# A graph network on one core: VectorE's turn in another order, node work in smaller pieces, the first steps rearranged

## The chip, the core and the metric

One core of a Trainium2 chip runs the whole network. The metric is the device time of one execution in microseconds; less is better. The engines are TensorE (PE in the profile; PEld is its weight load), VectorE (DVE), ScalarE (ACT), GpSimd (POOL) and SyncE (SP, whose queue issues most DMAs). They run side by side and meet through semaphores alone.

## What is computed

3125 nodes with 128 features each, 53,125 edges sorted by target. Four graph layers, each after a layer norm with ReLU:

```python
x[dst] gets, per edge:  relu([x[src], x[dst], edge_attr] @ mW1 + mb1) @ mW2 + mb2   # layer 0, then the mean
upd = relu([x, agg] @ uW1 + ub1) @ uW2 + ub2 + x ; layer norm with gamma, beta      # layer 0
x @ W1 + b1 + (segment_sum(x[src]) @ W2 + b2)                                       # layer 1
segment_sum(norm * (x @ W3)[src]) + bias      # layer 2, norm from edge weights and degrees
relu(0.9 * segment_sum(norm * x[src]) + 0.1 * x) + x                                # layer 3
```

## The kernel before

Nodes are 25 tiles of 128. The 53,125 edges are 104 quads of 512 (four columns of 128). Because the edges are sorted, the 512 targets of quad q lie in a window of 128 nodes that begins at first(q), about 30 q.

**Prologue (to about 30 us).** For the seven tile groups j, VectorE makes `variance(0, 0, x)(j)` and then `norm(0, 0)(j - 1)`; ScalarE makes the root between them; GpSimd scales the rows (`normed_rows`, L795, 25 operations); TensorE transposes them (T0) and multiplies with the first message weights (P, `make_P`); ScalarE reads P, and SP stores it as `p_rows` (L581). Meanwhile src, dst and weights of the edges are turned to float, packed and stored as `edges_in_order` by VectorE, GpSimd and SP, and `idx`, the source of every edge, comes to its place (L1235).

**Sweep (104 quads, loop `for q in range(NQ)` on every engine).** Layer 0 messages, and at the same time the dense blocks of the adjacency for layers 1 to 3:
- GpSimd gathers the rows of P for the sources of the edges: four indirect DMAs a quad (L811), into G, a ring of six quads (GS = 6). It waits only for the indices, for all of P stored, and from quad 6 on for the messages of quad q - 6.
- TensorE adds the gathered rows and the window's Q rows in PSUM (`pre`, L1736 and L1737), sums the messages by one-hots (`seg`, L1750), makes the Q window of quad q + 4 (L1723), and multiplies the operands of block step u = q - 4 (`blocks`, L1767 and L1769), one half before `seg` and one behind the Q window. It goes in this order: pre(q+1), blocks(u, 0), seg(q), Q window, a node piece if SLOT has one, blocks(u, 1).
- ScalarE reads messages (L951) and block products (L976, L981) and makes the rows of the windows (L957, L964).
- VectorE's turn q: add the sums of quad q - 1 into ST (L1284), copy the Q window out of PSUM (L1291), make the four one-hots of quad q + 1 (L1297), and the operands of block step u = q - 2: the mask (L1308, `iota_k` against the keys), the low keys (L1311), and three products of the mask with the parts of the weights (L1315). Then the steps of node pieces.
- The dense update of layer 0 is cut into 12 node pieces g (11 of two tiles in the sweep, the last of three tiles after it). SLOT gives each one three places: A at quad BEGIN + APART g, U two quads later, V five later; `piece_steps` lets variance, norm, residual, second norm and the low part follow the V by 2 to 7 quads. BEGIN is 57 and APART 4. At quad 46 one operation adds a bias to all of h (L1372), at quad 50 one to all of x (L1376), and degrees are made at quads 8, 16, 24, 32 (`block_degrees`) and 40.

```python
                if 8 <= q < 40 and q % 8 == 0:
                    block_degrees(q // 8 - 1)
                if q == 46:
                    bias_h0(0)
                if q == 50:
                    bias_x(B_BE)
```

**After the sweep.** The last piece is finished, GpSimd and others widen the count blocks from bytes (L502), and TensorE goes through the dense products of layers 1, 2 and 3 (L1896, L1911) to the end.

The order on each engine is the order in which the code is written; nothing reorders it.

## Time and profile before

| | us |
|---|---|
| median of 3 runs | 927.59 (924.33 to 929.0) |
| profiled execution | 929.52 |
| its span, first to last instruction | 927.7 |
| first gather to last gather starts | 25.82 to 600.15 |
| TensorE busy, share of span | 91% |
| VectorE busy | 68% |
| GpSimd busy | 56% |
| mean granted TensorE clock | 0.950 |

The profile is one execution, taken by the hardware. A row of the timeline gives start, length, engine, line, operation, output<-input, and in brackets how long the engine was idle before and what ended that. Numbers of buffers are left out of names: `room` is one large region that holds G, the Q rows, the operands and the window rows; `ps` is PSUM. TensorE's operations overlap, so its busy time says little; an engine that isn't the limit may idle at no cost.

### The profile page before, as it was taken

The numbers are of one execution on the slowest core, as the hardware profiler recorded it, in microseconds if no ns is written. First come the engines' busy times: TensorE is split into PE (matmuls) and PEld (weight loads), VectorE is DVE, ScalarE is ACT, GpSimd is POOL, SyncE is SP. The second block draws the span as 40 slices with busy tenths as digits, with TensorE's granted clock in tenths as the row PEclk, the third lists the DMA queues.
The fourth block names the chain that finished last, engine by engine and source line by source line (L and its number), as shares of the span: only waits on it lengthen the run. The fifth ranks groups of instructions, "written<-read, shape, count | busy, mean of one in ns | idle before, by whom it ended". The sixth has DMA issues, their size and how long they took to land.

```text
span 927.7 us, 18932 instructions
## 1 busy us (share of the span) xinstructions
PE 845.5 (91%) x6949; PEld 788.6 (85%) x6949; DVE 632.2 (68%) x1747; ACT 506.6 (55%) x1005; POOL 522.3 (56%) x496
## 2 busy tenths in 40 slices
PE   4549889898988789999989999989999999999996
PEld 4549888897988789998989999968899888898886
DVE  7659968976987777788987899748843311117663
ACT  4226666765766547677767878833444011114864
POOL 8677777777777787777777777753110000005110
PEclk9679989988999889999999999989999999999998
DMA  6624555656655655665655556582146877686500
GB/s 192 160 71 130 163 158 168 209 156 212 188 169 172 139 173 165 181 196 176 180 168 169 168 168 195 177 257 71 45 178 254 313 286 290 236 301 207 163 24 28
DMA packets 104977, 163.68 MB, mean 176 GB/s; under 512 B 14699, under 2 KB 65426, under 8 KB 104879
## 3 DMA queue, kind: packets, MB, share of 16 engines
q1 hardware_dynamic: 91230, 134.19, 43.7%
q0 software_dynamic: 13648, 28.21, 11.6%
q8 instruction: 59, 0.97, 0.4%
q14 instruction: 40, 0.32, 0.1%
HBM read 107.92 MB, written 54.43 MB: 175 GB/s over the span
## 4 chain that ended last, share of the span: by engine, by line
PE 49%; POOL 33%; issue 10%; DVE 3%; DMA 3%; ACT 1%; SPq 0%; DVEq 0%; POOLq 0%
POOL room L811 32%; PE ps L1911 14%; PE ps L1896 14%; PE ps L1736 4%; PE ps L1750 3%; PE ps L1737 3%; PE ps L1767 2%; PE ps L1769 2%; DMA room<-p_rows,idx 2%; PE ps L1880 2%; PE ps L1672 1%; POOL pair L811 1%; PE ps L1723 1%; DVE ST L1227 1%; PE ps L1783 1%
## 5 line engine op out<-in xcount | busy, mean ns | idle before, releaser
L811 POOL DMA_INDIRECT room<-p_rows,idx x416 | 440.1, 1058 | 129.1 <-issue 124.0
L1736 PE MATMUL ps<-room,ident 128*128 128x128 f32 x832 | 177.5, 297 | 44.0 <-DMA room<-p_rows,idx 39.0
L1736 PEld LDWEIGHTS ps<-room,ident 128*128 128x128 f32 x832 | 134.3, 203 | 47.2 <-DMA room<-p_rows,idx 41.7
L1737 PE MATMUL ps<-room 128*128 128x128 f32 x832 | 170.1, 289 | 0.0
L1767 PE MATMUL ps<-room 128*128 128x200 bf16 x784 | 161.5, 257 | 0.0
L1769 PE MATMUL ps<-room 128*128 128x100 bf16 x1568 | 160.9, 211 | 0.0
L1315 DVE TENSOR_TENSOR room<-room,Wp 128x800 bf16<-128x800 bf16 x294 | 152.3, 572 | 0.0
L1769 PEld LDWEIGHTS ps<-room 128*128 128x128 bf16 x1568 | 147.3, 99 | 4.6
L951 ACT ACTIVATE g<-ps 128x512 f32<-128x512 f32 x104 | 62.1, 597 | 134.4 <-PE ps L1737 134.4
L1737 PEld LDWEIGHTS ps<-room 128*128 128x128 f32 x832 | 135.3, 205 | 0.0
L1911 PE MATMUL ps<-room,h 128*128 128x256 f32 (+1 forms) x650 | 133.5, 367 | 0.0
L1911 PEld LDWEIGHTS ps<-room,h 128*128 128x128 f32 x650 | 117.9, 190 | 13.7
L1750 PE MATMUL ps<-g 128*128 128x128 f32 x832 | 119.6, 288 | 0.0
L976 ACT ACTIVATE room<-ps 128x400 uint8<-128x400 f32 x196 | 98.0, 500 | 38.0 <-PE ps L1769 34.6
L1896 PE MATMUL ps<-wide_room,parts 128*128 128x512 f32 (+2 forms) x520 | 108.4, 363 | 0.0
L1750 PEld LDWEIGHTS ps<-g 128*128 128x128 f32 x832 | 104.8, 198 | 0.1
L1896 PEld LDWEIGHTS ps<-wide_room,parts 128*128 128x128 f32 x520 | 88.9, 189 | 14.0
L981 ACT ACTIVATE room<-ps 128x400 f32<-128x400 f32 x196 | 98.5, 502 | 0.0
L1284 DVE TENSOR_TENSOR ST<-ST,ps 128x128 f32<-128x128 f32 x104 | 29.1, 280 | 95.1 <-PE ps L1723 61.2
L1297 DVE TENSOR_SCALAR g<-iota,dstT 128x128 f32<-128x128 f32 x416 | 92.7, 300 | 0.0
L904 ACT ACTIVATE sd<-mv,eps 128x2 f32<-128x2 f32 (+3 forms) x45 | 13.6, 302 | 132.6 <-DVE mv L1191 132.6
L957 ACT ACTIVATE room<-room,npio 125x512 bf16<-125x512 bf16 x104 | 75.7, 728 | 11.3 <-DMA room<-dst_row 11.3
(194 smaller groups left out, 1136.0 us busy)
## 6 DMA issues: line engine op xcount, KB each, us to landing
weight_blocks<-room SPq DMA_DIRECT2D x49, 800.0 KB
room<-weight_blocks SPq DMA_DIRECT2D x11, 3200.0 KB
room<-dst_row SPq DMA_DIRECT2D x52, 256.0 KB
count_blocks<-room SPq DMA_DIRECT2D x49, 200.0 KB
room<-count_blocks SPq DMA_DIRECT2D x6, 1600.0 KB
room<-p_rows,idx POOLq DMA_INDIRECT x416
first_c<-count_blocks SPq DMA_DIRECT2D x4, 1600.0 KB, 10.4
room<-weight_blocks SPq DMA_DIRECT2D x2, 2000.0 KB
```

The source lines that it names most:

```text
L811: return pool.indirect_dma_start(to, None, table, bass.IndirectOffsetOnAxis(ap=at, axis=axis))
L976: act.activation(cnt_out[:, u % OUTS, :, at16].rearrange("p h (b w) -> p b h w", w=4), of, ACT.Copy)\
L981: act.activation(w_out[:, u % OUTS, :, at16].rearrange("p h (b w) -> p b h w", w=4), of, ACT.Copy)\
L1297: last = dve.tensor_scalar(oh[:, q % OS, c, :], iota[:, :], dstT[:, q, c:c + 1], None, ALU.is_equal)
L1315: last = dve.tensor_tensor(mov[:, k, 1 + a, :, :, :], mov[:, k, 0, :, :, :], blocks_of(Wp[:, a, :], u, KCOLS), ALU.mult)
L1736: pe.matmul(to, ident[:, :], G[:, n % GS, c, :], start=True, stop=False)
L1737: last = pe.matmul(to, sT[:, n % TS, 128 * c:128 * c + 128], Qr[:, n % QS, :], start=False, stop=True)
L1750: last = pe.matmul(bank(2 + n % 2, 128), R[:, n % RS, c, :], oh[:, n % OS, c, :], start=c == 0, stop=c == 3)
L1767: pe.matmul(to.rearrange("p (a c) -> p a c", a=2), lo, mov[:, k, 0:2, i, :, t], start=True, stop=False)
L1769: weighed = pe.matmul(to[:, KCOLS:2 * KCOLS], lo, mov[:, k, 1 + a, i, :, t], start=False, stop=a == PARTS - 1)
L1896: last = pe.matmul(to, Hr[:, t, a, :], at[:, k, 0:n], start=a == 0 and t == 0, stop=a == 1 and t == NT - 1)
L1911: last = pe.matmul(bank(dense_bank(j))[:, at:at + 32 * c], h[:, t, :], ring_w[(2 * j + half) % 3][:, 0:c, t, :], start=t == 0, stop=t == N ...
```

## The change

What it does:
- **VectorE's turn** from quad 5 on (`turn_in_step`): add, mask, first product, Q copy, second and third product, the one-hots of quad q + 2 instead of q + 1, low keys. The mask waits, as before, until TensorE has multiplied both halves of step u - 3. Quads 0 to 4 keep the old turn, with the order mask, products, low keys.
- **Node pieces** from quad 27 on, seven quads apart (BEGIN 27, APART 7), the last three places at quads 97, 99 and 102 as before. The piece before the last has its V at 95 instead of 98.
- **Bias operations** by piece: 12 on h at quads 10, 12, ... 32, and 12 on x at quads 35, 37, ... 57, each 128x256 (the last 128x384). V of piece g waits for h's piece g, the residual for x's.
- **Degrees** at quads 6, 9, 12, 15 and 17; their store and load by SP at quads 20 and 23 instead of 49 and 52.
- **Prologue**: VectorE makes the window starts (sq) first; norm 0 follows variance 0 at once, norm 1 stands behind variance 2; the casts of src and dst, the subtraction and the packing stand between the variances of groups 3 to 6. GpSimd makes iota_k and iota_l ahead of the rows, and splits edge attributes ahead of the weights. ScalarE and not GpSimd sets the ones of the window rows (32 partitions), and turns dst_b to bf16 before the last P are read. TensorE transposes src before the last groups. SP stores dst_row before the last P, and the attributes before the edge windows.

```diff
-    BEGIN = 57
-    APART = 4
+    BEGIN = 27
+    APART = 7
+    BIAS_H, BIAS_X = 10, 35
+    DEGREES = 6
...
+                if j == NC - 2:
+                    sp.wait_ge(s_dr, 2)
+                    sp.dma_start(dst_row, dst_b).then_inc(s_drs, 16)
...
-            def block_operands(u):
+            def mask_operand(u):
                 if u >= SETS:
                     dve.wait_ge(s_wmm, 2 * (u - SETS + 1))
...
+            def turn_in_step(q):
+                u = q + 2 - LAG
+                add(q - 1)
+                if SLOT.get(q - 1, " ")[0] == "A":
+                    read_A_piece(SLOT[q - 1][1], slot_bank(q - 1))
+                if u < STEPS:
+                    mask_operand(u)
+                    weighed_operand(u, 0)
+                if q - 1 + LEAD < NQ:
+                    q_window(q - 1 + LEAD)
+                if u < STEPS:
+                    weighed_operand(u, 1)
+                    weighed_operand(u, 2)
+                if q + 2 < NQ:
+                    onehot(q + 2)
+                if u < STEPS:
+                    lo_operand(u)
...
+                if BIAS_H <= q < BIAS_H + 2 * NPC and (q - BIAS_H) % 2 == 0:
+                    bias_h0_piece((q - BIAS_H) // 2)
+                if BIAS_X <= q < BIAS_X + 2 * NPC and (q - BIAS_X) % 2 == 0:
+                    bias_x_piece((q - BIAS_X) // 2)
```

VectorE, one turn in the later sweep, before (add, Q copy, one-hots `g`, mask, low keys, products):

```order
L1284 TENSOR_TENSOR ST<-ST,ps 128x128
L1291 COPY room<-ps 125x128
L1297 TENSOR_SCALAR g<-iota,dstT 128x128 x4
L1308 TENSOR_TENSOR room<-iota_k,Kt 128x800
L1311 TENSOR_TENSOR room<-iota_l,LOt 128x1024
L1315 TENSOR_TENSOR room<-room,Wp 128x800 x3
```

The same turn after:

```order
L1299 TENSOR_TENSOR ST<-ST,ps 128x128
L1322 TENSOR_TENSOR room<-iota_k,Kt 128x800
L1331 TENSOR_TENSOR room<-room,Wp 128x800
L1306 COPY room<-ps 125x128
L1331 TENSOR_TENSOR room<-room,Wp 128x800 x2
L1312 TENSOR_SCALAR g<-iota,dstT 128x128 x4
L1335 TENSOR_TENSOR room<-iota_l,LOt 128x1024
```

The mask moved up to the add, the Q copy between the products, and the low keys from the second to the last place.

GpSimd in the prologue, from the ramp of keys (`pair`) to the first gathers, before:

```order
L779 IOTA pair 128x896
L779 IOTA npio 128x1
L800 MEMSET room 128x2048
L795 TENSOR_SCALAR h<-x,rs,nb 128x128 x25
L804 COPY room<-ST 104x624
L806 COPY room<-room 104x1024
L779 IOTA iota_k 128x200
L779 IOTA iota_l 128x256
L811 DMA room<-p_rows,idx 128x128 x12
```

After:

```order
L785 IOTA pair 128x896
L785 IOTA npio 128x1
L785 IOTA iota_k 128x200
L785 IOTA iota_l 128x256
L801 TENSOR_SCALAR h<-x,rs,nb 128x128 x25
L811 COPY room<-room 104x1024
L813 COPY room<-ST 104x624
L816 DMA room<-p_rows,idx 128x128 x12
```

The two iotas moved ahead of the 25 rows, the memset went to ScalarE, and the copies changed places.

VectorE at the end of the sweep, turns 102 and 103 (adds of quads 101 to 103, with what stands between them), before:

```order
L1284 TENSOR_TENSOR ST<-ST,ps 128x128
L1297 TENSOR_SCALAR g<-iota,dstT 128x128 x4
L1395 TENSOR_TENSOR h<-h,bc 128x256
L1396 TENSOR_TENSOR x<-x,h 128x256
L1188 BN_STATS bn<-x 128x6 x2
L1191 BN_AGGR mv<-bn 128x2 x2
L1284 TENSOR_TENSOR ST<-ST,ps 128x128
L1200 RECIPROCAL rs<-sd 128x2
L1203 SCALAR_TENSOR_TENSOR nb<-mv,rs 128x2
L1284 TENSOR_TENSOR ST<-ST,ps 128x128
```

After:

```order
L1299 TENSOR_TENSOR ST<-ST,ps 128x128
L1312 TENSOR_SCALAR g<-iota,dstT 128x128 x4
L1299 TENSOR_TENSOR ST<-ST,ps 128x128
L1442 TENSOR_TENSOR parts<-h,parts 128x2x128
L1299 TENSOR_TENSOR ST<-ST,ps 128x128 x2
```

The residual and second norm of piece 9 left these turns (they stand two to three turns earlier), and only its low part is between the last adds.

## Rows read from the trace of the kernel before

**Rows 1.** The page, busy us (share of the span) x instructions.

```profile
PE 845.5 (91%) x6949; PEld 788.6 (85%) x6949; DVE 632.2 (68%) x1747; ACT 506.6 (55%) x1005; POOL 522.3 (56%) x496
```

**Rows 2.** The page, the chain that ended last, by engine.

```profile
PE 49%; POOL 33%; issue 10%; DVE 3%; DMA 3%; ACT 1%; SPq 0%; DVEq 0%; POOLq 0%
```

**Rows 3.** The page's groups: busy us, mean ns of one, idle before, releaser.

```profile
L811 POOL DMA_INDIRECT room<-p_rows,idx x416 | 440.1, 1058 | 129.1 <-issue 124.0
...
L1284 DVE TENSOR_TENSOR ST<-ST,ps 128x128 f32<-128x128 f32 x104 | 29.1, 280 | 95.1 <-PE ps L1723 61.2
L1297 DVE TENSOR_SCALAR g<-iota,dstT 128x128 f32<-128x128 f32 x416 | 92.7, 300 | 0.0
```

**Rows 4.** Timeline of GpSimd, the first and the last gather: start, length in us.

```profile
25.82 1.46 POOL L811 DMA_INDIRECT room<-p_rows,idx  x1 [2.67 <-DVE idx L1235]
...
600.15 0.94 POOL L811 DMA_INDIRECT room<-p_rows,idx  x1 [0.31 <-issue]
```

**Rows 5.** The chain from 480 to 612 us, sums of four quads: start, length.

```profile
540.83 0.96 PE ps L1750 x8
...
557.19 0.96 PE ps L1750 x8
561.67 0.96 PE ps L1750 x8
```

**Rows 6.** Groups by line from 360 to 600 us, GpSimd and VectorE.

```profile
L811 POOL DMA_INDIRECT room<-p_rows,idx x180 | 185.7, 1032 | 54.9 <-issue 53.9 <-PE ps L1737 0.9
...
L1311 DVE TENSOR_TENSOR room<-iota_l,LOt 128x1024 bf16<-128x1024 bf16 x44 | 30.9, 702 | 1.5
```

**Rows 7.** Line 811 from 360 to 600 us: duration in ns, min/median/max.

```profile
L811 POOL DMA_INDIRECT room<-p_rows,idx x180: 940/945/1353, 359.6 to 598.9; - x180
```

**Rows 8.** Timeline from 440.9 us, GpSimd and VectorE.

```profile
440.94 0.57 DVE L1308 TENSOR_TENSOR room<-iota_k,Kt 128x800 bf16<-128x800 bf16 x1
440.98 1.35 POOL L811 DMA_INDIRECT room<-p_rows,idx  x1 [0.30 <-issue]
...
442.15 1.57 DVE L1315 TENSOR_TENSOR room<-room,Wp 128x800 bf16<-128x800 bf16 x3
442.63 0.95 POOL L811 DMA_INDIRECT room<-p_rows,idx  x1 [0.30 <-issue]
```

**Rows 9.** Timelines around the two bias operations, VectorE and GpSimd.

```profile
298.89 3.48 DVE L1372 SCALAR_TENSOR_TENSOR h<-h,bc 128x3200 f32<-128x3200 f32 x1
...
299.53 4.14 POOL L811 DMA_INDIRECT room<-p_rows,idx  x1 [0.30 <-issue]
...
323.69 3.67 POOL L811 DMA_INDIRECT room<-p_rows,idx  x1 [0.30 <-issue]
```

**Rows 10.** Timeline of the prologue, and from the DMA view the last store of P.

```profile
7.65 11.09 POOL L795 TENSOR_SCALAR h<-x,rs,nb 128x128 f32<-128x128 f32 x25 [2.79 <-DVE nb L1203]
...
17.51 0.48 DVE L1220 CAST ST<-ST 104x624 f32<-104x624 int32 x1
...
18.78 4.71 DVE L1227 CAST ST<-ST 104x624 f32<-104x624 int32 x1
...
21.98 0.53 SPq L581 DMA_DIRECT2D p_rows<-g  x1
...
24.64 0.88 DVE L1235 CAST idx<-ps 128x416 uint32<-128x416 f32 x1
...
p_rows<-g SPq DMA_DIRECT2D x1, 64.0 KB, 2.1
```

**Rows 11.** Timelines at the sweep's end, VectorE and TensorE.

```profile
607.88 2.42 DVE L1396 TENSOR_TENSOR x<-x,h 128x256 f32<-128x256 f32 x1
...
612.79 1.62 PE L1782 MATMUL ps<-ST,w_m 128*128 128x384 f32 x2 [3.23 <-issue]
```

**Rows 12.** Stretches: length, PE, PEld, DVE, ACT, POOL busy, PEclk, DMA share, GB/s.

```profile
612.00:619.00 7.00, 6.21 (x11) 3.48 (x12) 2.66 (x11) 2.36 (x6) 2.75 (x2) 0.52 1.10 346
```

155 lines of the change are left out of this document (92 added, 63 removed).

## The prediction

> **What bounds the kernel now.** I read the page from the top down. The busy shares first [rows 1]: VectorE is busy for 68% of the span, GpSimd for 56%, so no share names a limit. The chain that ended last does [rows 2]: GpSimd holds 33% of it and TensorE 49%. The page's costliest group says what GpSimd does there [rows 3]: 416 row gathers (line 811), 1058 ns each, and 129.1 us of idle time before them, nearly all of it "issue", not a wait for anybody. The first gather starts at 25.82 us and the last at 600.15 [rows 4]. So from 26 to 601 us GpSimd issues one gather after another (416, and 7 for the windows) and never waits, and everything else in the sweep runs behind it: the sweep ends when the gathers end. TensorE is close behind: it repeats a quad without a node piece in 4.48 us, 557.19 to 561.67, and four quads with one in 20.84, so 5.2 each [rows 5], against 4 x (1.032 + 0.305) = 5.35 us of GpSimd in the later sweep [rows 6].
>
> The reader should then see that the gather's time isn't its own. Its shortest and median are 940 and 945 ns, the mean 1032 [rows 6, 7]. What stretches it stands on VectorE. The gather of 440.98 starts 0.04 us after a mask (L1308, 440.94 to 441.51) and takes 1.35 us; 0.82 us after the mask's end the gather ends. The next gather, at 442.63, takes 0.95 although three products (L1315) run on without a break [rows 8]. The longest, 4.14 us, lies in the 3.48 us bias operation of L1372; the 3.67 us of 323.69 lie in the one of L1376, as long [rows 9]. So I read: about 0.13 us after it starts, a gather needs something that a VectorE operation with its operands in SBUF holds to its end; if such an operation runs then, the gather waits for that end and for that alone. Summed over all 423 gathers the stretch over 0.944 us is 47 us: (1.058 - 0.944) x 416 [rows 3] is 47.4. That sum is what this change can touch in the sweep.
>
> The Trainium skill, page "SBUF — State Buffer", section "Who interferes with whom", says that VectorE and GpSimd share one port pair, held for a whole instruction, and infers that `tensor_tensor` doesn't hold up descriptor generation, since it takes only the pair's read side. The row of the mask, a TENSOR_TENSOR, disagrees with that inference: 1.35 us and not 0.94 [rows 8]. What the forecast would be by it is the third rival.
>
> **The change part by part.**
> *The bias operations in pieces.* Two operations of 3.48 us become 24 of 128x256. They held gathers for 4.14 - 0.94 = 3.20 and 3.67 - 0.94 = 2.73 us [rows 9], 5.9 together. A piece lasts about 3.48 x 2/25 + 0.06 = 0.34 us, more than 0.2 of it after the point where a gather is caught; a gather asks every 1.25 us, so a piece costs at most 0.2 x 0.2 / 2 / 1.25 = 0.02 to 0.03 us, 0.7 for all. Net -5.2 us on the gather path.
>
> *The order of VectorE's turn.* Before, a turn has one row of 2.8 us without a gap: mask, low keys, three products, after the one-hots. Now it is add, mask, product, Q copy (from PSUM, which held no gather), two products, four one-hots, low keys. The work is the same; what changes is how a gather that was held meets the next operation. A held gather is let go at an operation's end, and the next one asks 0.944 + 0.305 = 1.249 us later. I walked both orders by hand with the durations of [rows 3, 6, 8] (mask and product 0.57, products 0.49 apart, low keys 0.70, one-hot 0.28 and 0.195 apart): first request at 21 phases, 0.06 us apart, each hold added up over the turn. Before: 0.37 us a turn on average, 0.03 to 0.79 by phase. That agrees with what is measured, (1032 - 944) ns x 4 = 0.35 a turn [rows 6]. After: 0.25, from 0 to 0.53. The main reason: low keys, the longest operation, were followed 1.249 us later by the third product, and now nothing follows them. The saving of the walk is 0.12 x 95 turns = 11.4 us. I take 10.5, since the node pieces still break the pattern. The bounds are the extreme phases for every turn: 0.35 x 95 = 33 us gained, (0.53 - 0.35) x 95 = 17 lost. I take a value near the mean because TensorE's 4.48 us and GpSimd's 1.249 have no common measure, so phases drift.
>
> *The new place of the mask* brings a wait: mask u needs both halves of blocks u - 3 multiplied, and the second half stands on TensorE behind the Q window that releases the add. It is twelve short bf16 products, well under a fifth of TensorE's quad. Queued behind it on VectorE are the Q copy and with it TensorE's sums, which need that copy only a whole quad later. VectorE has the room: it idled 95.1 us before the adds [rows 3], 0.9 a turn, and where it is behind the wait is zero. I cost it at nothing; the cover is that idle time, and if a turn (3.9 us of work, plus pieces and degree blocks) got longer than 5.3 us it would be gone. The four degree blocks (four operations on 896 elements each, some 4 us by the rate of L1372, 1.09 ns an element [rows 9]) stand at quads 6, 9, 12, 15 and not 8 to 32: VectorE falls behind there by some us, TensorE with it; GpSimd's rows are six quads (over 25 us) ahead of a stall. Nothing.
>
> *Node pieces from quad 27 on, seven quads apart.* TensorE's later quads get lighter: 5.2 us before with a piece in four quads, so 20.84 - 4 x 4.48 = 2.9 us a piece [rows 5], now 4.48 + 2.9/7 = 4.9 on average, under GpSimd's 5.28. Nothing on the path by itself, but the cover for the other gains: without it TensorE's 5.2 would eat most of them.
>
> *The prologue.* The first gather needs the indices (VectorE's cast at 24.64, 0.88 long) and all rows of P in memory. The indices were late because the cast of dst took 4.71 us beside GpSimd's copies and iotas, the same cast of src 0.48 [rows 10]; that goes, since the iotas and copies move away from it. But the P rows landed at 21.98 + 2.1 = 24.1 [rows 10], so only 25.8 - 24.3 = 1.5 us are there to gain, and the P path gets longer. Step by step: first norm at 7.1 instead of 7.5 (no second variance in front, four small operations of 0.8 in front); norm 1 now stands behind variance 2, so GpSimd's rows of tile group 1 start at 10.1 where they started at 9.4: about 1.1 us of waiting; four operations (two casts, the subtraction, the packing) now lie inside GpSimd's 25 rows of 0.44 and hold each one about 0.33 to 0.5, 1.6 us in all. GpSimd's rows end at 7.2 + 11.1 + 1.1 + 1.6 = 21.0 instead of 18.74 [rows 10], P lands 5.4 later, at 26.4, and the first gather starts at 26.8: +1.0 us. Bounds: all P waits hidden, -1.5; each cast held through a whole tile group as at 18.78, +4. SP stores dst_row before the last P and the edge windows after ea; those are wanted 10 us later and cost nothing.
>
> *The end of the sweep.* TensorE waits 3.23 us for the last add, and the last node piece starts at 612.79. VectorE was late because L1396, a step of piece 9, took 2.42 us, where 256 elements at 1.09 ns want 0.3 to 0.4; GpSimd's widening casts run then [rows 11]. Now the residual of piece 9 stands at turn 99, before those casts, so the last add follows TensorE: -2.5 us. The 3.2 us of idleness were followed by a clock of 0.52 from 612 to 619 (the lower of the two levels, 1.2 GHz) [rows 12], which cost some 3 us of TensorE's work there; with the gap down to about 1 us I expect half of that back: -1.5. Together -4.0 (0 to -6). The degrees of the last piece are now fetched after the last weight store instead of 8 us earlier; they should land at about 610, just in time.
>
> **Sum**: -5.2 - 10.5 + 1.0 - 4.0 = -18.7 us. The profiled execution took 929.52 us (span 927.7), so 910.8; the median of the three runs shown is 1.9 below it, 927.59, and 927.6 - 18.7 = 908.9. I say 909.
>
> **Rivals.** (1) *The order does nothing*: holds stay at 0.35 a turn, because the walk's gaps are filled with pieces and by VectorE's new wait. Then 908.9 + 10.5 = 919.4. For it: the pattern depends on tenths of a microsecond. Against: the walk gave the before right. (2) *TensorE takes over*: the gathers get faster than TensorE recovers from late landings; it would show as GpSimd waiting for messages or as a lag at the end of some 5 us, 914 to 916. Against: 4.9 to 5.28 us a quad. (3) *TENSOR_TENSOR doesn't hold a gather*: neither order nor pieces save anything, 908.9 + 10.5 + 5.2 = 924.6. This is the result by the page's inference; rows 8 and 9 leave little room. (4) *Slower*: GpSimd and VectorE lock at the bad phase, since TensorE starts VectorE's turn and the gather starts TensorE. At 0.53 us in every turn: 908.9 + 10.5 + 17 = 936. It decides once more than about 0.45 us a turn is held, all else as forecast; short of that the other gains outweigh it. For it: three quads in a row repeat a pattern in places. (5) *The prologue starves the casts*: +3, 912, within the forecast's own range.
>
> **How the numbers follow.** The forecast with (5), 900 to 915: 0.62. Rival 1 and mixtures of it: 0.17, ending 915 to 923. Rival 2: 0.07. Rival 3: 0.04. Rival 4: 0.06. Still faster than 900: 0.04. The range that leaves out 2 in 10: 900 to 922. A measurement of this kernel can tell about 0.5%, 4.6 us, from no change: faster means below 923.0. Faster: 0.62 + 0.15 + 0.07 + 0.04 = 0.88, less 0.03 for what I haven't thought of, 0.85; same 0.10; slower 0.05.
>
> **What would show it.** In the changed profile: gathers' mean near 1.02 us (all) and about 1.00 in the later sweep, none over 2 us; first gather at 26 to 28 us, last at about 585; GpSimd's idle time before gathers still "issue"; last add right behind the last sums and the last piece within 1.5 us of them; no half clock at the sweep's end, or a shorter one. A mean of 1.03 or more in the later sweep says rival 1, over 1.08 rival 4. GpSimd waiting for TensorE's message products (L1737 before) in the sweep says rival 2. A first gather after 29 us says the prologue's part is wrong.

## The result, and the profile after

The changed kernel takes **916.09 us** (median of four runs, 911.1 to 917.49) against 926.75 for the kernel before on the same chip (median of four, 924.33 to 929.0): a ratio of 0.987, 95% interval 0.9842 to 0.9899. The forecast was 909. Faster is right, and 916 lies in the range; of the 18.7 us that the sum promised, 10.7 came. The profiled execution took 917.49 us, span 915.6.

The page of the changed kernel, first the busy times (us, share of the span, instructions), then the chain that ended last by engine, then the group of the gathers (line 816 now: busy us, mean ns of one, idle time before them):

```profile
PE 833.4 (91%) x6949; PEld 777.7 (85%) x6949; DVE 633.4 (69%) x1769; ACT 506.6 (55%) x1006; POOL 507.5 (55%) x495
...
PE 43%; POOL 37%; issue 11%; DMA 4%; DVE 3%; ACT 1%; SPq 1%; DVEq 0%; POOLq 0%
...
L816 POOL DMA_INDIRECT room<-p_rows,idx x416 | 426.5, 1025 | 132.7 <-issue 125.6
```

Against [rows 1 to 3]: VectorE and TensorE do the same work, GpSimd's gathers are shorter by 13.6 us (440.1 to 426.5), 1025 ns each instead of 1058. They are still issued one behind the other.

The later sweep alone, line 816 from 360 to 600 us (min/median/max in ns), to be read against [rows 6, 7]. The mean there is 994 ns, before it was 1032:

```profile
L816 POOL DMA_INDIRECT room<-p_rows,idx x178: 940/947/1352, 359.8 to 589.7; - x178
...
L816 POOL DMA_INDIRECT room<-p_rows,idx x178 | 176.9, 994 | 54.3 <-issue 53.6 <-PE ps L1797 0.6
```

GpSimd's timeline in the prologue, from its last rows of the norm to the first gather (start and length in us, what ended the idle time before it), then SyncE's stores, and from the DMA view what P's last store took from issue to landing:

```profile
16.56 4.37 POOL L801 TENSOR_SCALAR h<-x,rs,nb 128x128 f32<-128x128 f32 x9 [0.37 <-DVE nb L1213]
...
28.92 1.17 POOL L816 DMA_INDIRECT room<-p_rows,idx  x1 [6.20 <-DMA p_rows<-g]
...
24.34 0.48 SPq L591 DMA_DIRECT2D dst_row<-room  x1
24.86 0.37 SPq L587 DMA_DIRECT2D p_rows<-g  x1
...
p_rows<-g SPq DMA_DIRECT2D x1, 64.0 KB, 3.2
```

The indices were ready at 21.7 us. The gathers now wait for P, and they begin at 28.92 and not at 25.82 [rows 4].

The end of the sweep: GpSimd's last gather, TensorE's first product of the last quad, and its first product of the last node piece:

```profile
589.70 0.94 POOL L816 DMA_INDIRECT room<-p_rows,idx  x1 [0.30 <-issue]
...
597.65 0.45 PE L1796 MATMUL ps<-room,ident 128*128 128x128 f32 x2
...
603.63 0.88 PE L1842 MATMUL ps<-ST,w_m 128*128 128x384 f32 x2 [1.29 <-DMA rest<-degrees]
```

**Where the time went.** Four stretches add up to the difference of the spans, 927.7 - 915.6 = 12.1 us. Up to the first gather: 25.82 to 28.92, +3.1. From there to the end of the last gather: 575.3 to 561.7, -13.6. From there to TensorE's last quad: 601.1 to 604.8 before, 590.6 to 597.6 now, +3.3. From there to the end: 322.9 to 318.0, -4.9.

### The profile page after: what moved, and what is told of

Its sections match the earlier page's. It is cut to its first block, busy times and chain, and to the rows that moved or that the text cites. A ratio compares the mean times of both kernels' runs of the same rounds, so it can differ in the third digit from the quotient of the medians.

```text
span 915.6 us, 18961 instructions
## 1 busy us (share of the span) xinstructions
PE 833.4 (91%) x6949; PEld 777.7 (85%) x6949; DVE 633.4 (69%) x1769; ACT 506.6 (55%) x1006; POOL 507.5 (55%) x495
## 3 DMA queue, kind: packets, MB, share of 16 engines
q0 software_dynamic: 13648, 28.21, 12.1%
## 4 chain that ended last, share of the span: by engine, by line
PE 43%; POOL 37%; issue 11%; DMA 4%; DVE 3%; ACT 1%; SPq 1%; DVEq 0%; POOLq 0%
POOL room L816 36%; PE ps L1971 14%; PE ps L1956 13%; PE ps L1796 3%; DMA room<-p_rows,idx 2%; PE ps L1797 2%; PE ps L1810 2%; PE ps L1940 2%; PE ps L1827 2%; PE ps L1829 2%; PE ps L1731 1%; POOL pair L816 1%; DMA ST<-in_src 0%; ACT h L917 0%; DVE nb L1213 0%
## 5 line engine op out<-in xcount | busy, mean ns | idle before, releaser
L816 POOL DMA_INDIRECT room<-p_rows,idx x416 | 426.5, 1025 | 132.7 <-issue 125.6
L1796 PE MATMUL ps<-room,ident 128*128 128x128 f32 x832 | 175.0, 294 | 49.0 <-DMA room<-p_rows,idx 48.2
L1796 PEld LDWEIGHTS ps<-room,ident 128*128 128x128 f32 x832 | 131.8, 200 | 52.7 <-DMA room<-p_rows,idx 41.7
L1331 DVE TENSOR_TENSOR room<-room,Wp 128x800 bf16<-128x800 bf16 x294 | 159.2, 570 | 3.4
L1827 PE MATMUL ps<-room 128*128 128x200 bf16 x784 | 159.0, 255 | 0.0
L1829 PE MATMUL ps<-room 128*128 128x100 bf16 x1568 | 158.2, 209 | 0.0
L1829 PEld LDWEIGHTS ps<-room 128*128 128x128 bf16 x1568 | 145.5, 98 | 4.1
L1810 PE MATMUL ps<-g 128*128 128x128 f32 x832 | 117.5, 285 | 0.7 <-DVE room L1306 0.6
L1810 PEld LDWEIGHTS ps<-g 128*128 128x128 f32 x832 | 102.6, 194 | 1.0 <-ACT g L961 1.0
L1312 DVE TENSOR_SCALAR g<-iota,dstT 128x128 f32<-128x128 f32 x416 | 100.6, 319 | 0.0
L1827 PEld LDWEIGHTS ps<-room 128*128 128x128 bf16 x784 | 77.6, 99 | 3.9 <-issue 3.6
```

Of the source, the lines that this page charges most:

```text
L816: return pool.indirect_dma_start(to, None, table, bass.IndirectOffsetOnAxis(ap=at, axis=axis))
L1312: last = dve.tensor_scalar(oh[:, q % OS, c, :], iota[:, :], dstT[:, q, c:c + 1], None, ALU.is_equal)
L1331: dve.tensor_tensor(mov[:, k, 1 + a, :, :, :], mov[:, k, 0, :, :, :], blocks_of(Wp[:, a, :], u, KCOLS), ALU.mult)
L1796: pe.matmul(to, ident[:, :], G[:, n % GS, c, :], start=True, stop=False)
L1810: last = pe.matmul(bank(2 + n % 2, 128), R[:, n % RS, c, :], oh[:, n % OS, c, :], start=c == 0, stop=c == 3)
L1827: pe.matmul(to.rearrange("p (a c) -> p a c", a=2), lo, mov[:, k, 0:2, i, :, t], start=True, stop=False)
```

## The experiments

A word on how holds are counted below: all time of the 423 gathers over 0.944 us each, from the trace of the profiled execution, and put down to the VectorE operation that was in flight 0.13 us after the gather began (its moment of asking). Rows of operations that follow each other without a break overlap by about 0.08 us; where two are in flight, the hold is put down to the first. Before: 47.6 us, of it products 14.7, mask 10.4, low keys 7.8, one-hots 1.4, the two bias operations 5.9. After: 34.0, of it low keys 10.9, products 9.3, mask 4.1, one-hots 2.1, biases 0.6. The low keys' 10.9 are explained further down: 7.2 of them lie behind the low keys' own end.

### The order alone

The kernel before with the new turn, all else as before.

```
-  add, window copy, A piece, one-hots(q+1), mask, low keys, products
+  add, A piece, mask, product, window copy, two products, one-hots(q+2), low keys
```

> The kernel before with VectorE's turn alone in the new order (from quad 5 on). Theory A, a held gather meets the next operations by the order: the holds by mask, products, low keys and one-hots fall from 34 to about 26 us, the mean gather from 1058 to about 1038 ns, the last gather ends near 593 instead of 601, and the time is 6 to 8 us below the kernel before; less, if TensorE's 5.2 us a quad in the late sweep takes over. Theory B, the order is indifferent and the changed kernel's fewer holds are chance or come from the spread pieces: mean 1055 to 1060, time as before.

Measured: 912.27 us (ratio 0.985, interval 0.9803 to 0.9896), holds 33.5 us, first gather 26.32.

```profile
L812 POOL DMA_INDIRECT room<-p_rows,idx x416 | 426.0, 1024 | 129.2 <-issue 124.7
```

The order alone brings some 14 us, at least as much as the whole change (10.7), and twice the 6 to 8 that were expected; the mean gather is 1024 ns where 1038 was expected. It doesn't touch the biases (two gathers of over 3.8 us stand beside them), the pieces or the prologue, and its gathers are as short as those of the changed kernel, 1024 ns against 1025. So the rest of the change gave nothing on balance. Whether it cost something can't be told from the times alone (909.78 to 914.21 us here, 911.1 to 917.49 for the changed kernel).

### The low keys last, in the old turn

The kernel before; the low keys go behind the products, nothing else moves.

```
                 link(mask)
-                low keys
                 for a in range(PARTS):
                     product(a)
+                low keys
```

> The kernel before with one edit in VectorE's turn: mask, three products, low keys, so that the low keys stand last and nothing else moves. Theory A by the same walk over phases: 0.55 us held a turn against 0.41 for the order before, so holds rise by about 13 us, mean gather near 1090 ns, time 8 to 13 us above the kernel before. Rival C, the gain of the new turn is only that the longest operation stands last with nothing behind it: holds fall by some us, time 3 to 8 us below. Theory B: no difference.

Measured: 949.55 us (ratio 1.0235, interval 1.0171 to 1.03), holds 67.6 us, of them products 28.0 and mask 17.3.

```profile
L811 POOL DMA_INDIRECT room<-p_rows,idx x416 | 460.0, 1106 | 129.3 <-issue 121.0
```

The same five operations, in the same place, one of them moved by three: +23 us. The walk over phases has the sign right and the size of the difference too small. In the later sweep the gathers' mean here is 1082 ns, so (1.082 - 0.944) x 4 = 0.55 us are held a turn, just what the walk gave for this order; but it gave 0.41 for the order before, where 0.35 is measured. Putting the longest operation last doesn't by itself make a turn good: here it stands last and the kernel is slower. By the walk, what counts is where the next gather's request falls.

### The whole old prologue

The changed kernel with the prologue of before.

```
-            count_up(iota_k ...), count_up(iota_l ...)   # ahead of the rows
+            count_up(iota_k ...), count_up(iota_l ...)   # behind the rows and copies
-            last P store behind dst_row; ones by ScalarE; second variance ahead of norm 1
+            as in the kernel before
```

> The changed kernel with the whole prologue of the kernel before (all engines). If the new prologue costs what its first gather shows (28.92 instead of 25.82), the first gather is back at 25.8 and the time 3 us below the changed kernel, near 913. Rival: what starts earlier is lost again at TensorE, which isn't ready for the first rows sooner; then the time stays at 916.

Measured: 912.45 us (ratio 0.9846, interval 0.9796 to 0.9897), first gather at 26.39, last gather's end 589.46. The first gather is 2.5 us earlier than in the changed kernel and the time 3.6 less, though the single times overlap (910.05 to 915.06 and 911.1 to 917.49). The first gather is the firmer sign: in the profiles of the kernels with the old prologue it starts at 25.82 to 26.90, with the new one at 28.86 to 28.98. The new prologue costs 2 to 3 us.

### P's last store alone

The changed kernel; SyncE waits for all of P before it stores anything else.

```
-                if j == NC - 2:
-                    sp.wait_ge(s_dr, 2)
-                    sp.dma_start(dst_row, dst_b).then_inc(s_drs, 16)
+            sp.wait_ge(s_pt, 16 * NC)
+            sp.wait_ge(s_dr, 2)
+            sp.dma_start(dst_row, dst_b).then_inc(s_drs, 16)
```

> The changed kernel; SyncE waits until all of P has landed before it stores the other small arrays (dst_row, the edge attributes, the packed edges). Theory: the last P store landed 4.0 us after its issue at 24.86 instead of 2.1 because of the stores issued beside it; alone it lands near 27, the first gather starts at 27.0 instead of 28.9, and the time falls by 1.9 us. Rival: the landing is as slow without them, first gather 28.5 or later, same time. Danger: dst_row and the edge rows come 3 us later, and if they are needed before then the first messages are late and the gain is gone; first gather tells this apart from the time.

Measured: 914.79 us (ratio 0.9871, interval 0.9835 to 0.9907); first gather at 28.87. SyncE's timeline, GpSimd's, and the DMA view:

```profile
24.78 0.51 SPq L587 DMA_DIRECT2D p_rows<-g  x1
28.01 0.33 SPq L591 DMA_DIRECT2D dst_row<-room  x1
...
28.87 1.17 POOL L816 DMA_INDIRECT room<-p_rows,idx  x1 [5.72 <-DMA p_rows<-g]
...
p_rows<-g SPq DMA_DIRECT2D x1, 64.0 KB, 3.2
```

The theory falls. With no store beside it, P's last store still takes 3.2 us; SyncE, which waits for the same landing, sees it at 28.0, and the gather begins 0.86 us later. So the neighbours are not the cause. (The 4.0 us in the expectation are the time from issue to first gather, not to the landing.) Two things are left: the store is issued late (24.8 against 21.98 in [rows 10]), because P's last tile group is late, and from issue to first gather it takes 4.1 us. Why the landing takes 3.2 us here and 2.1 in [rows 10] stays open. It isn't the new prologue alone: with the old one the same store took 2.1 us in seven profiles and 3.3 in one, that of the kernel with the low keys last, whose first gather started at 26.90; with the new one it took 2.8 to 3.2 in five.

### The old order put back

The changed kernel; the turn is in the old order, but one-hots still two quads ahead and the mask still signals a semaphore of its own that the first product waits for.

```
+                add, window copy, A piece, one-hots(q+2)
                 mask_operand(u)
+                lo_operand(u)
                 weighed_operand(u, 0)
-                ...
```

> The changed kernel with the turn back in the old order (add, Q copy, one-hots, mask, low keys, products; one-hots still two quads ahead). Theory A: holds go up by about 8 us, mean gather from 1025 to about 1045 ns, time 5 to 8 us above the changed kernel's 916, so near 923. Theory B: 916.

Measured: 1027.66 us (four runs, three of them at 1022.92 to 1029.63 and one at 1050.33; ratio 1.1088, interval 1.1019 to 1.1157), holds 143.7 us. Over 100 us slower than the expectation, and than the kernel before, with the same operations in the same order. The timelines of VectorE and of GpSimd at 470 us say how:

```profile
469.98 0.57 DVE L1322 TENSOR_TENSOR room<-iota_k,Kt 128x800 bf16<-128x800 bf16 x1
470.47 0.69 DVE L1335 TENSOR_TENSOR room<-iota_l,LOt 128x1024 bf16<-128x1024 bf16 x1
471.07 1.54 DVE L1331 TENSOR_TENSOR room<-room,Wp 128x800 bf16<-128x800 bf16 x3
...
470.62 2.80 POOL L816 DMA_INDIRECT room<-p_rows,idx  x1 [0.30 <-issue]
```

The gather asks while the low keys run. It isn't let in at their end, 471.16, nor at the end of the first or the second product: it ends at 473.42, which is 0.81 us after the third product's end, 472.61. In 56 gathers of this run, over 2 us each, 119 us go. The prediction's reading, "the gather waits for that end and for that alone", is not the whole truth. In the kernel before, VectorE waited for the mask before it issued the low keys (0.03 us of idleness between L1308 and L1311); here it doesn't. The next three runs are about that.

### No break behind the mask, in the kernel before

```
-                link(mask)
-                low keys
+                mask.then_inc(s_mask, 1)
+                low keys
+                dve.wait_ge(s_mask, u + 1)
                 products
```

> The kernel before with one change: the mask signals a semaphore of its own, and the first product waits for it, instead of VectorE waiting for the mask before it issues the low keys. So the low keys follow the mask with no break between them, and mask, low keys and three products run in one unbroken chain; the order is that of before. In the run in which the old order was put back into the changed kernel (the same unbroken chain), gathers that asked in the mask or the low keys were held to the end of the third product, 2.4 to 3.6 us each. Theory H (the missing break is the cause): the same happens here, holds of 110 to 150 us in place of before's 48, last gather near 690 to 705, time 1000 to 1030. Rival I (it was the one-hots made two quads ahead, or the window copy ahead of them, that did it): holds stay near 48 us, time 924 to 932.

Measured: **1038.77 us** (ratio 1.1194, interval 1.1117 to 1.1272), holds 151.8 us, 60 gathers over 2 us. Theory H. The timelines show one turn of VectorE and three gathers of GpSimd, one a turn; a row with x3 or x4 is that many operations:

```profile
383.82 0.28 DVE L1292 COPY room<-ps 125x128 f32<-125x128 f32 x1
384.03 0.86 DVE L1298 TENSOR_SCALAR g<-iota,dstT 128x128 f32<-128x128 f32 x4
384.81 0.57 DVE L1309 TENSOR_TENSOR room<-iota_k,Kt 128x800 bf16<-128x800 bf16 x1
385.29 0.68 DVE L1313 TENSOR_TENSOR room<-iota_l,LOt 128x1024 bf16<-128x1024 bf16 x1
385.89 1.54 DVE L1318 TENSOR_TENSOR room<-room,Wp 128x800 bf16<-128x800 bf16 x3
...
381.10 3.42 POOL L812 DMA_INDIRECT room<-p_rows,idx  x1 [0.30 <-issue]
384.83 3.42 POOL L812 DMA_INDIRECT room<-p_rows,idx  x1 [0.30 <-issue]
388.55 3.42 POOL L812 DMA_INDIRECT room<-p_rows,idx  x1 [0.30 <-issue]
```

The gather of 384.83 asks as the mask starts; the products end at 385.89 + 1.54 = 387.43, and the gather at 388.25, again 0.82 later. When it is let go the next asks in the next turn's mask: one gather a turn instead of three. A wait that looks like a waste of 0.03 us of VectorE was worth 112 us.

### The break put back into the old order

```
                     mask_operand(u)
+                    dve.wait_ge(s_mask, u + 1)
                     lo_operand(u)
```

> The changed kernel with the old order of the turn (add, window copy, one-hots two quads ahead, mask, low keys, products) as in the run before of that kind, and one wait more: VectorE waits for the mask before it issues the low keys, as the kernel before did. Theory H (the missing break held gathers through the whole chain): back from 1027.7 to about what the old order is worth with the rest of the change, 920 to 930, no gather over 2 us but beside the degree sums. Rival I (one-hots and window copy): stays over 1000.

Measured: 925.08 us (median of ten, ratio 0.9981, interval 0.9955 to 1.0007), holds 45.6 us, no gather over 2 us.

```profile
L816 POOL DMA_INDIRECT room<-p_rows,idx x416 | 438.1, 1053 | 132.6 <-issue 123.4
```

Theory H, and at the same time the answer to the first question: with the break in place, the old order in the changed kernel is 9 us slower than the new order (925.1 against 916.1), and the rest of the change brings nothing measurable.

### The break ahead of the mask

The unbroken kernel, with a wait for the one-hots before the mask. Mask, low keys and products still follow each other without a break.

```
+                dve.wait_ge(s_oh, u + 4)
                 mask.then_inc(s_mask, 1)
                 low keys
                 dve.wait_ge(s_mask, u + 1)
                 products
```

> The kernel with the unbroken chain, in the order of before, and one wait added: VectorE waits for the one-hots before it issues the mask, so that there is a break ahead of the mask instead of behind it; mask, low keys and three products still run with no break between them, and the first product still carries its wait for the mask. In the runs so far the long holds (2.4 to 3.6 us) came where a one-hot ran into the mask with no break; a chain that began after a break let gathers in at the ends of its operations, in the kernel before and in the kernel that only gathers. Theory L (the two-input operations that follow one-hots without a break are one stretch for a waiting gather, and a break at their head ends that): no gather over 2 us but beside the degree sums, holds 45 to 60 us, time 925 to 940. Rival J (the missing break behind the mask, or the wait that the first product carries, does it whatever stands ahead): holds over 110 us, time over 1000.

Measured: 941.85 us (ratio 1.0161, interval 1.0128 to 1.0193), 2 us above what theory L expected; holds 59.9 us. Three gathers are over 2 us, two of them beside the bias operations. VectorE, then GpSimd:

```profile
245.77 0.58 DVE L1310 TENSOR_TENSOR room<-iota_k,Kt 128x800 bf16<-128x800 bf16 x1
246.26 0.68 DVE L1314 TENSOR_TENSOR room<-iota_l,LOt 128x1024 bf16<-128x1024 bf16 x1
246.86 1.54 DVE L1319 TENSOR_TENSOR room<-room,Wp 128x800 bf16<-128x800 bf16 x3
...
246.39 1.37 POOL L812 DMA_INDIRECT room<-p_rows,idx  x1 [0.31 <-issue]
```

The gather asks 0.26 us into the low keys, and the products follow with no break; it ends at 247.76, 0.82 after the low keys' end (246.94). All 26 gathers held in the low keys here were let in so. In the two kernels with no break anywhere (the old order put back, and this one without its wait), all 52 that asked in the first 0.29 us of the low keys were kept out to the end of the products. Theory L: a break at the head of the chain does what the break in its middle did, and rival J falls. What a waiting gather can't pass is a run of two-input operations that was entered from a one-hot without a break. It can pass the end of one if VectorE stood still, here for 0.1 us ahead of the mask.

All thirteen profiles of the network bear this out. Take the gathers that were held after they had asked in a mask, low keys or product with another operation close behind. Where the run had begun after a break, 934 were let in at the end of the operation in which they asked, and 2 were not. Where a one-hot stood in the run, 214 of 504 were kept beyond it. The two exceptions stand at the same place (quad 2) of the two kernels without a break behind the mask; here it is this one, the third over 2 us, in VectorE's and GpSimd's timelines:

```profile
73.50 1.53 DVE L1319 TENSOR_TENSOR room<-room,Wp 128x800 bf16<-128x800 bf16 x3
...
73.54 2.79 POOL L812 DMA_INDIRECT room<-p_rows,idx  x1 [0.30 <-issue]
```

It asks in the first product and ends at 76.33, so it was let in about 75.51, behind the third product's end (75.03), though VectorE had stood still 0.03 us ahead of the run, before a small operation on one element. Theory L doesn't cover it.

The 15 us that this kernel still loses against the one before are products (28.9 us of holds for 14.7): another meeting of the same turn with the gathers, not long holds.

### One kind of work at a time

A kernel with gathers on GpSimd and one kind of operation on VectorE; nothing of the reference is computed.

```
+            for s, (turn, times) in enumerate(stages):
+                dve.wait_ge(s_gat, 16 * NG * s)
+                dve.memset(acc[:, :], float(s)).then_inc(s_end, 1)
+                for _ in range(times):
+                    turn()
```

> A kernel that computes nothing of the reference: eleven stages of 24 single gathers of 128 rows on GpSimd, each beside one kind of VectorE work: none; the mask alone with a wait after each; three products in a chain; mask, low keys, three products with no break, the first product carrying a wait for the mask; the same chain with products that read other data and carry no wait; the same with VectorE waiting after the mask; three products of which the second carries a wait that was met long before; four one-hots; an addition with one input from PSUM; an addition of two fp32 inputs in SBUF; a reduction. Theory J (a gather that asks beside a two-input operation is let in at that operation's end, unless the operation behind it follows without a break and carries a wait; then it is held to the end of the chain): quiet 0.94 us a gather; lone mask, products, free chain and broken chain none over 1.5 us; the chain whose first product waits holds gathers of 2 to 3.5 us, and the three products with a wait in the second hold gathers up to 2.0. Rival K (it is the length of the unbroken chain, not the wait): the free chain of five holds as long as the chain with the wait, and the three products hold none over 1.5 either way. One-hots and the addition from PSUM hold nothing (0.94 to 1.0), by both; the fp32 addition and the reduction hold up to their own length.

Line 62 (the gathers) by stage, ns min/median/max: three products in a chain; the unbroken chain of five with its wait; one-hots; an addition with one input in PSUM; an addition of two inputs in SBUF; a reduction.

```profile
L62 POOL DMA_INDIRECT G<-in_x,idx x24: 940/1274/1281, 69.0 to 104.1; - x24
...
L62 POOL DMA_INDIRECT G<-in_x,idx x24: 940/1052/1394, 107.1 to 138.7; - x24
...
L62 POOL DMA_INDIRECT G<-in_x,idx x24: 938/946/988, 252.5 to 281.6; - x24
L62 POOL DMA_INDIRECT G<-in_x,idx x24: 940/944/947, 284.8 to 313.5; - x24
L62 POOL DMA_INDIRECT G<-in_x,idx x24: 938/1067/1129, 316.6 to 350.6; - x24
L62 POOL DMA_INDIRECT G<-in_x,idx x24: 940/944/947, 353.7 to 382.4; - x24
```

No gather over 1.4 us in any stage. J falls as worded. K's wording for the stages is met (the longest gather is 1.390 us beside the free chain, 1.394 beside the one with the wait), but only because neither chain held a gather past an operation's end; a long unbroken chain alone doesn't do it either. The chain of five is entered after a break here, and one wait carried by the second of three products changed nothing (24 gathers, median 1274 ns with it and without); that is what led to theory L. The test of the chain is thin: gathers and chains fell into step, and of 22 gathers beside it only 2 asked in the mask or the low keys, the others in products. It also lacks what theory L is about, since no stage puts one-hots ahead of a chain, and its one-hots are bf16 where those of the network are fp32.

The rest is as expected but for the reduction, which I had said holds a gather up to its length. It holds none, though it was in flight nearly all the time (26 of 1.2 us, back to back). The same for the addition from PSUM. The Trainium skill says of `tensor_reduce` on trn2 that it never contends (page "SBUF — State Buffer", section "Who interferes with whom"); this stage agrees, 944 ns.

The lone mask held none either, and that says little: gathers (1.25 us apart) and masks (0.61) fell into step, nearly all gathers began as a mask began, and so asked within its first 0.14 us. Products show the same: a gather that asked 0.12 or 0.13 us into one was not held, one that asked 0.25 us into it was. So an operation doesn't hold from its first moment.

The stage of products shows how firmly the two engines lock. One chain of three and its wait takes 1.58 us, and 19 of the 20 gathers beside such chains were held 0.33 us, so that one gather, too, takes 1.58:

```profile
70.32 1.27 POOL L62 DMA_INDIRECT G<-in_x,idx  x1 [0.30 <-issue]
71.90 1.28 POOL L62 DMA_INDIRECT G<-in_x,idx  x1 [0.30 <-issue]
73.48 1.28 POOL L62 DMA_INDIRECT G<-in_x,idx  x1 [0.30 <-issue]
```

### The low keys in two halves

The kernel with the order alone; two operations of 128x512 for one of 128x1024.

```
+                for i in range(0, NW, 2):
+                    last = dve.tensor_tensor(sta[:, u % SETS, i:i + 2, :, :], ...)
```

> The kernel before with the new order of the turn alone, and the low keys made by two operations of half the size. Holding theory: a gather that asks beside a two-input operation waits for that operation's end, so two of 0.38 us hold half as much as one of 0.68. In the run with the order alone the low keys held 8.9 us: now 4 to 5.5, last gather 3 to 5 us earlier than 587.6, time 1 to 4 us below that run's 912.3. Rival (the extra operation of VectorE a quad, or the chain it forms, costs as much): same or slower. If a gather is held through both halves, nothing is gained.

Measured: 916.44 us (ratio 0.987, interval 0.9833 to 0.9907), holds 38.0 us, low keys 10.1 of them (8.9 in one piece). Fallen: the rival (same or slower) is right. The halves take 0.41 us each. All 55 gathers that were held there asked in the second half, 45 of them some 0.28 us into it, and waited 0.13 to 0.15 us for its end. Each is held less, but more of them are: 55 against 49.

### The biases

First the changed kernel with whole bias operations, at quads 10 and 35.

```
-                bias_h0_piece((q - BIAS_H) // 2) ... bias_x_piece((q - BIAS_X) // 2)
+                the whole of h at q == BIAS_H, the whole of x at q == BIAS_X
```

> The changed kernel with the two bias operations whole again (one of 25 tiles each, at quads 10 and 35) in place of pieces. Theory (pieces hold gathers less: the two whole operations held 5.9 us before, the pieces 0.6): holds up by 5 us, last gather near 595 to 596, time 920 to 922 against 916.1. Rival (the pieces cost what they save, because they lengthen the turns in which they stand and move the other operations against the gathers): 914 to 917.

Measured: 915.37 us (ratio 0.9858, interval 0.9831 to 0.9884), holds 32.8 us. The rival is right in the time. The two whole operations held one gather each, 3.4 us (beyond the low keys in which it asked) and 2.8, 6.2 together; the pieces of the changed kernel held 4.3, counted as below. That the sum of holds is no higher with the whole ones (32.8 for 34.0) is due to other operations, which the gathers met at other points. So the pieces brought nothing that can be measured. Then the reverse: new order and bias pieces, with the old prologue and the node pieces where they were.

```
-    BEGIN = 27
-    APART = 7
+    BEGIN = 57
+    APART = 4
```

> The new order and the biases in pieces, with the prologue of before and the node pieces where they stood before (every 4 quads from quad 57). Theory (the biases in pieces save 4 us of holds; spreading the pieces gained nothing): 907 to 910, below the 912.3 of the order alone. Rival (spreading the pieces gains, or the bias pieces save nothing): 911 to 914.

Measured: 912.06 us (904.42 to 916.83; ratio 0.9805, interval 0.974 to 0.987). Two of its four runs are at 904 and 907, two at 917, so it can't be told from the order alone (912.27) or from the old prologue (912.45). Its profiled run is one of the long ones, and shows the end of the sweep as before: TensorE waits for the last add, and from 598 to 612 the granted clock is 0.68 and 0.81.

```profile
599.98 1.47 PE L1832 MATMUL ps<-ST,w_m 128*128 128x384 f32 x2 [2.57 <-issue]
...
598.00:604.00 6.00, 4.02 (x7) 1.71 (x8) 2.56 (x10) 1.44 (x4) 3.93 (x2) 0.68 0.92 275
604.00:612.00 8.00, 8.00 (x33) 6.04 (x32) 2.87 (x14) 3.12 (x8) 2.84 (x2) 0.81 1.10 340
```

From TensorE's last quad to the end that run takes 322.2 us, the kernel with the order alone 317.3 (0.43 us of waiting there, clock 1.00), before 322.9. So some 5 us hang on whether the last add is in time. Three kernels, all without the new prologue, have medians some 4 us below the changed kernel; the scatter of single runs is as large.

## Why the prediction was right or wrong

**The order: right in mechanism, and the largest term.** Forecast -10.5 for the order and -5.2 for the biases, -15.7 of gather time; measured -13.6, and the gathers' mean in the later sweep is 994 ns where "about 1.00" was forecast. Held a turn, that is (0.994 - 0.944) x 4 = 0.20 us; the walk had 0.25. By the time of the runs the order is worth 14.3 us in the kernel before and 9.0 in the changed one (925.08 to 916.09), on either side of the 10.5. The time up to the own end of mask, products, low keys and one-hots fell from some 34 us to 19 (mask 10.4 to 4.1, products 14.7 to 9.3, low keys 7.8 to 3.7), -15. That is more than forecast, and the low keys gained by standing last, as the walk had said. By standing last alone they don't: in the old turn that cost 23 us.

**The step that was wrong: "for that end and for that alone".** It holds in the kernel before, where VectorE stands still behind the mask. It doesn't hold for a run entered from the one-hots, and the new order has such a run: the low keys, and whatever follows them. "Now nothing follows them" is true of the bare turn alone. Timelines of VectorE and GpSimd at 301 us, where a piece of the bias follows:

```profile
301.04 0.68 DVE L1335 TENSOR_TENSOR room<-iota_l,LOt 128x1024 bf16<-128x1024 bf16 x1
301.64 0.41 DVE L1411 TENSOR_TENSOR x<-x,bc 128x256 f32<-128x256 f32 x1
...
301.53 1.35 POOL L816 DMA_INDIRECT room<-p_rows,idx  x1 [0.30 <-issue]
```

The gather ends at 302.88, 0.83 us after the piece's end (302.05), not after the low keys' (301.72). This row alone doesn't decide: the gather asks at 301.66, in the 0.08 us in which both rows are in flight, and 17 of the 19 such gathers of this kernel ask so, 0.01 us after the next operation began. The rule as the prediction has it, applied to the piece, would explain them too. Products that follow one another speak against that: 30 gathers of this kernel asked in the first of two products 0.04 to 0.07 us after the second had begun, and were let in at the first one's end, and none was kept for the second.

Summed over the changed kernel, gathers that asked in the low keys were kept 7.2 us beyond the low keys' own end: 3.7 by pieces of the biases (ten gathers), 1.6 by the degree blocks, 1.7 by steps of node pieces, 0.2 by a small sum. In the kernel before no gather was kept beyond the low keys' end. This is where the gain of the biases went: the two whole operations held 5.9, the pieces 0.6 by themselves and 3.7 behind the low keys, so the term is -1.6 and not -5.2 by the trace; by the time, whole or in pieces made no difference (915.37 and 916.09). A break between the one-hots and the low keys, or between the low keys and the piece, might get part of the 7.2 us back; it wasn't tried.

The change also moves VectorE's wait for its own mask: it stands no longer behind the mask whatever follows, but ahead of the first product. The prediction doesn't speak of this; what it put at nothing is the mask's wait for TensorE. In the new order the moved wait costs nothing, because the first product stands right behind the mask and the break stays. In the old one the same edit costs over 100 us, a danger that the prediction didn't see and that the new order happens to avoid. That is luck.

**The prologue: mis-sized, +3.1 instead of +1.0.** GpSimd's rows end at 20.93, as forecast (21.0). P was to land at 26.4 and the first gather to start at 26.8. Three steps failed: the last store was issued at 24.86, landed after 3.2 us and not 2.1, and the gather started 0.86 us after that. In [rows 10] the last of these could not be seen, because the first gather there waited for the indices and not for P; the forecast left 0.4 us for it. The 2.1 us were taken from one profile for a step that takes 2.1 to 3.3 in others. It isn't SyncE's order that costs it, as P's last store alone showed.

**The end of the sweep: about right.** -4.9 against -4.0, with no half clock behind it; the last piece starts 1.29 us behind the last sums, and waits for its degrees, not for the add. The stretch from TensorE's last quad to the end shows where this gain lives. Before it takes 322.9 us, and 323.0 to 323.2 in the three others made from it without the new turn. With the new places of the pieces it takes 317.8 to 320.0 in six kernels, two of them with the old order. With the new order and the old places it takes 317.3 in one, 322.2 and 322.4 in two. So the gain goes with the places of the pieces; the order alone brings it at times.

**The lag of TensorE: not in the sum.** 7.0 us behind the last gather instead of 3.7. In the last 30 us of its sweep TensorE waits once for rows that land late, and the clock falls behind it. TensorE's waits from 560 to 600 us, its row there, and the windows (PEclk is the third number from the end):

```profile
PE ps L1796 <- DMA room<-p_rows,idx: 4.0, 1, 4.0
...
570.98 0.58 PE L1796 MATMUL ps<-room,ident 128*128 128x128 f32 x1 [3.97 <-DMA room<-p_rows,idx]
...
570.00:576.00 6.00, 5.02 (x29) 4.87 (x29) 1.44 (x7) 1.20 (x2) 4.47 (x6) 0.50 0.20 47
576.00:590.00 14.00, 14.00 (x140) 13.11 (x139) 10.64 (x35) 10.22 (x23) 10.65 (x12) 0.98 0.48 145
```

At a clock of 0.50 (the lower level, 1.2 GHz) TensorE falls behind, and with under 30 us of sweep left it doesn't catch up. This is rival 2's sign, "a lag at the end of some 5 us", and its time, 914 to 916. But GpSimd waited 0.6 us for TensorE in the later sweep, so TensorE has not taken over. The other kernels with the new order lag by 2.6 to 6.3 us.

Late landings are no news: from 60 to 600 us TensorE waited for rows 16 times in this kernel (35.5 us in all) and 15 times in the kernel before (37.2); what is new is one so near the end. Why rows land late was not tried. Nor is it the only way to a lag: the kernels with the low keys in halves (6.3 us) and with the biases in pieces and the node pieces every four quads (5.3) show no such wait from 540 us on and a granted clock of 1.00 from 540 to 590. There TensorE works without a pause, as rival 2 has it, but this was not followed up.

**The other rivals.** That the order does nothing (1) is out by the 14 us of the order alone. That a TENSOR_TENSOR doesn't hold a gather (3) is out by 1274 ns beside products; the Trainium skill's inference on descriptor generation (page "SBUF — State Buffer", section "Who interferes with whom") doesn't hold here. Slower (4) was not this kernel, but an order can cost as much: +23 us with the low keys last. With a run that a gather can't enter, which no rival foresaw, it is +112. The casts of the prologue (5) were not starved: those of src and dst took 0.51 and 0.47 us (that of dst 4.71 before).

**The number.** Of the terms, the gathers came 2.1 us short, the prologue cost 2.1 more, the lag of TensorE added 3.3, and the end of the sweep gave 0.9 more than forecast: 12.1 us between the two profiles in place of 18.7, and 10.7 between the medians. That 916 lies between 900 and 922 is the merit of a wide range as much as of the sum: one part, the order, made the whole gain, and by its time it gave more than forecast in the kernel before.

## What to carry to other kernels

Where GpSimd's indirect gathers set the pace, VectorE's two-input operations are part of their price, and the order of VectorE's turn is worth per cents (here -9 to -14, and +23 us) with no work changed. Count what a gather meets in a trace, but don't add holds up as savings, since the next request moves with each hold. And look at each place where VectorE stands still between operations before it is tidied away: a wait that left 0.03 us of idleness was the door through which the gathers came in.

The time of a store from issue to landing, read off one profile, is not the price of a path through that store: it differed by 1.2 us from kernel to kernel, and the first gather began another 0.86 us after the landing. Where something in the trace waits for the store alone, take the time to its start.

## What the runs showed of the hardware

- A gather of 128 rows by GpSimd takes 0.944 us and 0.305 until the next, with nothing beside it. In these traces it goes on 0.81 to 0.82 us after it is let in.
- It is held by operations of VectorE with both inputs in SBUF (median 1274 ns beside products, 1067 beside an fp32 addition) and, by up to 0.04 us, by bf16 one-hots (in the network, fp32, typically up to 0.07: gathers of 1.01 us); not by an addition with one input in PSUM nor by a reduction (944 both). So the engines don't meet through semaphores alone, as the first section has it.
- The Trainium skill has the port pair of the two engines held for a whole instruction (page "SBUF — State Buffer", section "Who interferes with whom"). The runs agree where the run of operations began after a break (934 of 936 held gathers). Where it was entered from one-hots without a break, a gather stayed out for up to five instructions, 3.42 us. Not every one: in the two kernels with such runs 36 of 68 that asked in the mask stayed out to the end, and 76 of 86 that asked in the low keys.
- In the mask the moment of asking decides, the same way in both kernels. All 24 that asked 0.14 to 0.187 us after its start stayed out, all 15 from there to 0.21 were let in at its end, and so were all 17 at 0.37 to 0.40; all 11 at 0.50 to 0.56 stayed out (the one left, at 0.36, did too). Why it goes so is open, and so is why the one-hots matter.
- The two engines fall into step: in the stage with products 19 of 20 gathers were held by the same 0.33 us, and in the unbroken kernel gathers at 381.10, 384.83 and 388.55 by the same 2.48.
